# A macaron block's weight preparation on one core: constants between weight tiles, x in four loads, W2 pieces in pair order

## What is computed

```python
x = x + 0.5 * ffn(layernorm(x), W1, W2, W3)
x = x + attention(layernorm(x), qkv_w, ...)   # linear attention with decay, 16 heads of 32, chunks of 128
x = x + 0.5 * ffn(layernorm(x), W1, W2, W3)

def ffn(x, W1, W2, W3):                        # W1, W3: 2048 x 512, W2: 512 x 2048
    hidden = silu(x @ W1.T) * (x @ W3.T)
    return fwht(hidden) @ W2.T                 # fwht: normalised Walsh-Hadamard transform over 2048
```

## Time and profile before

| | |
|---|---|
| median of three runs | 2354.49 us (2353.8 to 2356.52) |
| profiled execution, its own time | 2355.63 us |
| span of its records | 2353.9 us |
| TensorE matmuls busy | 2336.4 us (99%), 12407 instructions |
| VectorE busy | 1232.0 us (52%), 2211 instructions |
| ScalarE busy | 692.4 us (29%), 1164 instructions |
| GpSimd busy | 149.8 us (6%), 126 instructions |
| moved by DMA | 196.83 MB, 299457 packets |

### The profile page before, as it was taken

How to read it: one execution, slowest core, us unless ns; L and a number is a source line. 1 busy time by engine, 2 the same in 40 slices (tenths; PEclk the granted TensorE clock), 3 DMA queues, 4 the chain that set the end, 5 groups by cost and what they waited for, 6 DMA issues and landing times.

```text
span 2353.9 us, 31017 instructions
## 1 busy us (share of the span) xinstructions
PE 2336.4 (99%) x12407; PEld 1120.7 (48%) x12407; DVE 1232.0 (52%) x2211; ACT 692.4 (29%) x1164; POOL 149.8 (6%) x126
## 2 busy tenths in 40 slices
PE   8999999999999999999999999999999999999999
PEld 4444444444544454445444444445444544544444
DVE  6577555654565446546554465544664455445212
ACT  6645233222222222223223222222232213221211
POOL 0190000000000000000000000000000000000000
PEclk9999999999999999999999999999999999999999
DMA  8856622331243212422042223421432224131200
GB/s 218 229 152 175 157 86 64 89 86 50 68 77 107 72 28 82 103 75 64 28 138 51 54 81 90 99 54 28 121 68 85 50 54 99 31 87 36 65 25 19
DMA packets 299457, 196.83 MB, mean 84 GB/s; under 512 B 231600, under 2 KB 256176, under 8 KB 295472
## 3 DMA queue, kind: packets, MB, share of 16 engines
q1 hardware_dynamic: 299024, 194.31, 31.6%
q10 hardware_dynamic: 288, 0.52, 0.1%
HBM read 84.68 MB, written 54.53 MB: 59 GB/s over the span
## 4 chain that ended last, share of the span: by engine, by line
PE 94%; DVE 3%; issue 1%; ACT 1%; DMA 1%; SPq 0%; POOL 0%; DVEq 0%; ACTq 0%; POOLq 0%
PE d_bank L1437 27%; PE l_bank L1417 27%; PE g_bank L1417 26%; PE a_bank L1472 5%; PE a_bank L1532 2%; PE a_bank L1455 2%; PE a_bank L1483 1%; PE a_bank L1514 1%; PE a_bank L1519 1%; PE a_bank L1497 1%; DVE work L1146 1%; DVE work L1126 0%; DMA w1t<-kT 0%; PE a_bank L1521 0%; PE d_bank L1391 0%
## 5 line engine op out<-in xcount | busy, mean ns | idle before, releaser
L1437 PE MATMUL d_bank<-w2t,work 128*128 128x512 f16 x2940 | 671.9, 379 | 0.0
L1437 PEld LDWEIGHTS d_bank<-w2t,work 128*128 128x128 f16 x2940 | 284.7, 98 | 332.4 <-DVE work L1146 0.6
L1126 DVE SCALAR_TENSOR_TENSOR work<-l_bank,l_scale,work 128x512 f32<-128x512 f32 x256 | 191.8, 749 | 468.4 <-PE l_bank L1417 468.4
L1417 PE MATMUL g_bank<-xt,w1t 128*128 128x512 f16 x1536 | 354.1, 380 | 3.6 <-DMA w1t<-kT 3.6
L1417 PE MATMUL l_bank<-xt,w3t 128*128 128x512 f16 x1536 | 352.4, 379 | 0.0
L857 ACT ACTIVATE work<-g_bank,g_scale 128x512 f32<-128x512 f32 x256 | 175.4, 685 | 490.1 <-PE g_bank L1417 488.2
L876 ACT CAST work<-work 128x512 f16<-128x512 f32 x232 | 143.3, 618 | 562.0 <-DVE work L1126 561.1
L1417 PE MATMUL l_bank<-work,w3t 128*128 128x512 f16 x1344 | 308.4, 379 | 0.2 <-DVE work L1126 0.2
L1417 PE MATMUL g_bank<-work,w1t 128*128 128x512 f16 x1344 | 308.3, 379 | 0.0
L1417 PEld LDWEIGHTS g_bank<-xt,w1t 128*128 128x128 f16 x1536 | 148.3, 98 | 177.9 <-DMA w1t<-kT 4.6
L1417 PEld LDWEIGHTS l_bank<-xt,w3t 128*128 128x128 f16 x1536 | 148.1, 98 | 173.0 <-issue 0.2
(11 more groups left out here) (227 smaller groups left out, 1791.1 us busy)
## 6 DMA issues: line engine op xcount, KB each, us to landing
work<-parts_dram SPq DMA_DIRECT2D x192, 128.0 KB, 2.7
x_dram<-work SPq DMA_DIRECT2D x16, 1024.0 KB, 4.2
work<-x_dram SPq DMA_DIRECT2D x11, 1024.0 KB, 6.6
parts_dram<-q_parts SPq DMA_DIRECT2D x32, 256.0 KB, 2.0
parts_dram<-k_parts SPq DMA_DIRECT2D x32, 256.0 KB, 2.2
norm_dram<-cent SPq DMA_DIRECT2D x32, 256.0 KB, 2.0
w2t<-in_L_ffn_W_dram SPq DMA_DIRECT2D x30, 256.0 KB, 3.2
xin<-in_L_attn_x_dram SPq DMA_DIRECT2D x7, 1024.0 KB, 8.4
```

Of the source, the lines that this page charges most:

```text
L1126: nc.vector.scalar_tensor_tensor(out=hfull, in0=l_bank[:], scalar=l_scale[:, j:j + 1], in1=gate, op0=ALU.mult, op1=ALU.mult).then_inc(hful ...
L1417: ins = nc.tensor.matmul(dst[:], wt[:, wp, k, P * j:P * (j + 1)], src[:, xp, k, :], start=(k == 0 and wp == xp), stop=(k == KT - 1 and wp ...
L1437: ins = nc.tensor.matmul(d_bank[t][:], parts[:, hp, P * t:P * (t + 1)], w2t[:, j, wp, :], start=(j == 0 and hp == wp), stop=(j == HT - 1 a ...
```

## The change

The Hadamard constants and `diag` are made by a new step `consts` in three parts, in slots 4, 6 and 8 of the first pass, from other buffers. The next x is loaded in four pieces behind tiles 7, 9, 11 and 13. Its statistics move from slots 7 to 13 to slots 9 to 15, and the six parts of its normalisation from slots 14 to 24 to slots 16 to 26. The scales of chunks 2 and 3 are made one by one, `wsum` 2 comes behind `wprep` 2, `wsum` 3 behind `gate` 0. Batch 0's turns use four banks and four buffers, and `warm` 4 between them is gone. The W2 pieces get new slots, pieces 1 and 2 of each four change places, and pair 0 waits for pieces 0 to 13 only, pair 4 for the last two.

```diff
+        bits_p, bits_j = cent[:, 1, 0:P].bitcast(I32), cent[:, 1, P:2 * P].bitcast(I32)
+        first_cent = zt[:].rearrange("p a k t -> p (a k t)").bitcast(F32).rearrange("p (t d) -> p t d", t=TT)
...
+        turn_bank = a_bank + d_bank[2:4]
...
-        SCALED = [slice(0, 1), slice(1, 2)] + [slice(j, j + 2) for j in range(2, HT, 2)]
+        SCALED = [slice(j, j + 1) for j in range(4)] + [slice(j, j + 2) for j in range(4, HT, 2)]
...
             steps += [("stat", key), ("wscale", 0), ("prep", (key, 0)), ("prep", (key, 1)), ("wprep", 0), ("prep", (key, 2))]
-            steps += [("turn", (key, 0)), ("prep", (key, 3)), ("turn", (key, 1)), ("wprep", 1), ("warm", 4)]
-            steps += [("turn", (key, t)) for t in range(2, TT)] + [("warm", 8), ("wsum", 2), ("wscale", 1), ("wprep", 2), ("wprep", 3)]
-            steps += [("wsum", 3), ("wscale", 2), ("wprep", 4)]
+            steps += [("prep", (key, 3)), ("turn", (key, 0)), ("turn", (key, 1)), ("turn", (key, 2)), ("wprep", 1)]
+            steps += [("turn", (key, 3)), ("warm", 8), ("wscale", 1), ("wprep", 2), ("wsum", 2), ("wprep", 3)]
+            steps += [("wscale", 2), ("wprep", 4)]
             own = {}
             flies = [("fly", (t, st)) for t in range(KT) for st in range(BUTTERFLIES)]
             for t in range(TT):
-                add(own, 7 + 2 * t, [("rows", (("ffn1", 1), t))])
+                add(own, 9 + 2 * t, [("rows", (("ffn1", 1), t))])
             for i, part in enumerate(norm_steps(("ffn1", 1))):
-                add(own, 14 + 2 * i, part)
+                add(own, 16 + 2 * i, part)
+            for part, at in enumerate((4, 6, 8)):
+                add(own, at, [("consts", part)])
             for j in range(HT):
                 steps += [("gate", j)]
                 if j < HT - 2:
                     steps += [("wprep", 2 * j + 5)]
+                if j == 0:
+                    steps += [("wsum", 3), ("wscale", 3)]
                 if j < HT - 4:
                     steps += [("wsum", j + 4)]
                 steps += own.get(2 * j, []) + [("lin", j)]
                 if j < HT - 4 and j % 2:
-                    steps += [("wscale", (j + 5) // 2)]
+                    steps += [("wscale", (j + 7) // 2)]
...
-            splits = (14, 16, 18, 20, 21, 22, 23, 24, 25, 25, 26, 26, 27, 27, 28, 28)
+            splits = (14, 16, 17, 18, 20, 21, 22, 23, 24, 25, 25, 26, 27, 28, 29, 30)
...
+        CHUNK_ORDER = (0, 2, 1, 3)
...
-                    if arg == 5:
-                        sp.dma_start(x_next, x[1].rearrange("(t p) d -> p t d", p=P)).then_inc(x_next_loaded, 16)
+                    if arg in (7, 9, 11, 13):
+                        t = (arg - 7) // 2
+                        sp.dma_start(x_next[:, t, :], x[1, P * t:P * (t + 1), :]).then_inc(x_first[t], 16)
...
-                    t, q = divmod(arg, CHUNKS)
+                    t, q = arg // CHUNKS, CHUNK_ORDER[arg % CHUNKS]
...
+                elif step == "consts":
+                    if arg == 0:
+                        dve.wait_ge(pool_const, 4)
+                        link(nc.vector.tensor_tensor(bits_p, bits_p, bits_j, ALU.bitwise_and))
+                        link(nc.vector.tensor_scalar(bits_j, bits_p, 4, None, ALU.logical_shift_right))
+                        link(nc.vector.tensor_tensor(bits_p, bits_p, bits_j, ALU.bitwise_xor))
+                        link(nc.vector.tensor_scalar(bits_j, bits_p, 2, None, ALU.logical_shift_right))
+                    elif arg == 1:
+                        link(nc.vector.tensor_tensor(bits_p, bits_p, bits_j, ALU.bitwise_xor))
+                        link(nc.vector.tensor_scalar(bits_j, bits_p, 1, None, ALU.logical_shift_right))
+                        link(nc.vector.tensor_tensor(bits_p, bits_p, bits_j, ALU.bitwise_xor))
+                        link(nc.vector.tensor_scalar(bits_p, bits_p, 1, None, ALU.bitwise_and))
+                    else:
+                        nc.vector.tensor_copy(hadamard_f32, bits_p).then_inc(dve_const, 1)
...
-                            pe.wait_ge(w2_turned[b], 16 * KT * CHUNKS // 4)
+                            pe.wait_ge(w2_turned[b], 16 * (KT if b < 2 else KT - 1))
...
                         pe.wait_ge(w2_final_lo, 2 * (i - 3))
+                        if i == 4:
+                            for b in (2, 3):
+                                pe.wait_ge(w2_turned[b], 16 * KT)
...
                     key, t = arg
-                    b = take(step, arg)
+                    b, _ = filled(step, arg)
                     pe.wait_ge(ln_norm, TT * NORM[key] + (t + 1))
                     for k in range(KT):
-                        ins = nc.tensor.transpose(a_bank[b][:, P * k:P * (k + 1)], cent[:, t % 3, P * k:P * (k + 1)], ident[:])
+                        ins = nc.tensor.transpose(turn_bank[t][:, P * k:P * (k + 1)], first_cent[:, t, P * k:P * (k + 1)], ident[:])
```

More of the change, by code:

```diff
@@ L768, in _ @@
             nc.scalar.activation(tiny[:, 15:16], ident[:, 0:1], ACT.Silu)
-            act.wait_ge(dve_const, 1)
-            squares = [(dve_const, 1)]
+            squares = []
             def sum_squares(v, out, done):
-                act.wait_ge(*squares[-1])
+                if squares:
+                    act.wait_ge(*squares[-1])
                 nc.scalar.activation(junk[:], v, ACT.Square, accum_out=out).then_inc(done, 1)
@@ L964, in inverse_norm @@
                                                ALU.mult, ALU.add)
-            dve.wait_ge(pool_const, 4)
-            ip, ij = junk[:, 2 * P:3 * P].bitcast(I32), junk[:, 3 * P:4 * P].bitcast(I32)
-            link(nc.vector.tensor_tensor(ip, ip, ij, ALU.bitwise_and))
-            for shift in (4, 2, 1):
-                link(nc.vector.tensor_scalar(ij, ip, shift, None, ALU.logical_shift_right))
-                link(nc.vector.tensor_tensor(ip, ip, ij, ALU.bitwise_xor))
-            link(nc.vector.tensor_scalar(ip, ip, 1, None, ALU.bitwise_and))
-            nc.vector.tensor_copy(hadamard_f32, ip).then_inc(dve_const, 1)
-            dve.wait_ge(dve_const, 1)
-            nc.vector.tensor_scalar(hadamard[:, 0, :], hadamard_f32, -2.0, 1.0, ALU.mult, ALU.add)
-            nc.vector.tensor_scalar(hadamard[:, 1, :], hadamard_f32, 2.0, -1.0, ALU.mult, ALU.add).then_inc(dve_const, 1)
-            link(nc.vector.memset(diag[:], 0.0))
-            for h in range(HG):
-                nc.vector.memset(diag[HD * h:HD * (h + 1), HD * h:HD * (h + 1)], SCORE_SCALE)
+            dve.wait_ge(pool_const, 2)
             for step, arg in STEPS:
@@ L986, in _ @@
                     n = f.n
+                elif step == "consts":
[12 more added lines that the diff above has]
+                        nc.vector.tensor_copy(hadamard_f32, bits_p).then_inc(dve_const, 1)
+                        dve.wait_ge(dve_const, 1)
+                        nc.vector.tensor_scalar(hadamard[:, 0, :], hadamard_f32, -2.0, 1.0, ALU.mult, ALU.add)
+                        nc.vector.tensor_scalar(hadamard[:, 1, :], hadamard_f32, 2.0, -1.0, ALU.mult, ALU.add).then_inc(dve_const, 1)
+                        link(nc.vector.memset(diag[:], 0.0))
+                        for h in range(HG):
+                            nc.vector.memset(diag[HD * h:HD * (h + 1), HD * h:HD * (h + 1)], SCORE_SCALE)
                 elif step == "wscale":
@@ L1151, in _ @@
                     if kind == "ffn1":
-                        if batch == 0:
-                            dve.wait_ge(x_first[t], 16)
+                        if batch < 2:
+                            dve.wait_ge(x_first[t], 16 * (batch + 1))
                         else:
-                            dve.wait_ge(*((x_next_loaded, 16 * batch) if batch < 4 else (x_loaded, 16 * batch)))
+                            dve.wait_ge(*((x_next_loaded, 16 * (batch - 1)) if batch < 4 else (x_loaded, 16 * batch)))
                     elif kind == "qkv":
@@ L1234, in _ @@
                         dve.wait_ge(ln_lo, TT * (m - 1) + t)
-                    to = centred if m else cent[:, t % 3]
+                    to = centred if m else first_cent[:, t]
                     if key[0] == "qkv":
```

12 lines of the change are left out of this document (6 added, 6 removed).

## The result

The changed kernel took 2359.64 us, the median of 19 runs (2358.55 to 2360.81), against 2354.49 for the kernel before in as many runs on the same chip: ratio 1.002, 95% interval 1.0013 to 1.0027. That is 5.1 us slower. The profiled execution has a span of 2358.9 us against 2353.9. Both profiled executions are 1.0 to 1.1 us above the medians (2360.68 and 2355.63), so the two traces can be compared term by term, but a wait that only some executions have can be in them.

The account below looks back on a forecast made before the run. TensorE, busy 2336.4 of 2353.9 us, was taken as the bound. Terms -4.2 - 5.0 + 10.9 + 1.7 = +3.4 us on the median of 2354.49 gave 2357.9 us, range 2353.5 to 2362.0.

Parts of the forecast that it names:

- the likeliest case: Second pass: `gate` 0 stalls 10.9 us for the transpose behind the W2 loads; 2357.9 us in all, chance 58%.
- Parts 1 and 2: First pass: x in four loads ends the `gate` 3 stall and slow clock, `lin` 1 starts 0.5 later; gain 4.2 us.
- Constants: First pass, VectorE: 3.66 us of constants ahead of `lin` 2, 3 and 4 fit and cost nothing, 0.3 us otherwise.
- Part 3: End of second pass: W2 pieces in new slots let `lin` 15 and pair 0 start on time; gain 5.0 us.
- by `lin` 10 both orders hold the same work: Second pass, VectorE: one more W2 piece stands behind `lin` 8, but old and new slots are level by `lin` 10.
- Part 4: Second pass, `gate` 0: normalisation two slots later puts its transpose behind 4.8 MB; stall 10.9, clock 1.7, loss 12.6 us.
- The rule weighed: Transpose before `gate` 0: about 2.0 us plus bytes at 436 GB/s lands it at 110.1, sum 2352.
- my row: Transpose before `gate` 0: lands at 115.9, from s's landing at 114.9 plus 1.0 us.
- the early drain: Before `gate` 0: rows and s don't hold the transpose, landing 112.3, stall 7.3; 2354.3 us, no change; chance 8%.
- the transpose that isn't held: Before `gate` 0: the transpose is issued ahead of the W2 loads, only gains left; 2345.3 us; chance 8%.
- The deeper backlog: Before `gate` 0: transpose lands at 117.3, clock at 1.2 GHz for two stretches; +6.5, 2361.0 us; chance 26%.

Follow-up runs that it names:

- the first run: The changed kernel with the last split of batch 1's normalisation in slot 25 in place of 26; 2349.18 us, ratio 0.9978.
- the run with the rows behind: The changed kernel with only the three rows and s issued behind the last split's transpose, W2 loads still ahead of it; 2357.48 us, ratio 1.0011.

## Why the prediction was right

The forecast of 2357.9 us was 1.7 below the median of 2359.64, inside its range, and the likeliest case is the one that happened. The sign and the place were right. That the number came so near is in part luck: the gains were taken 0.6 + 1.1 = 1.7 us too large and the loss 1.7 us too large, which cancels; what is left is a term of 1.7 us that was missing.

- **Parts 1 and 2** (gain 4.2): 3.6 in this trace. The wait for `gate` 3 went, as said. `lin` 0 waited 1.1 us for tile 1, of which the forecast says nothing: its ScalarE part stands behind the third turn and the tile is issued at 15.57 in place of 14.92. `lin` 1 came at 26.32 and not 25.75; VectorE's hfull 0 behind the scales of chunk 3 was the bound, as named. The size also rested on one execution whose wait, with its slow clock, was worse than in others: alone, x in four loads gave 2.2 us, not 4.7.
- **Constants:** nothing waits for them, as said.
- **Part 3** (gain 5.0): 3.9. The failed step is "by `lin` 10 both orders hold the same work". In the new slots VectorE does 4, 5, 7 and 9 pieces ahead of hfull 9 to 12, in the old ones 3, 4, 6 and 8; only ahead of hfull 13 both have 12. The extra piece falls in the time in which GpSimd is at work and a piece can cost VectorE 1.75 us in place of 0.75. VectorE falls behind and stays so until the butterflies end; with pieces 2 to 12 back in the old slots most of it went. `lin` 15 and pair 0 were on time, as said.
- **Part 4** (loss 12.6): 9.6 + 1.3 = 10.9; alone 11.8. The mechanism held in each trial. The landing was predicted 12.3 us behind the transpose's issue (115.9 for 103.57) and came 10.0 behind it. I took s's 11.8 us from the trace of before, which were 9.9 in the changed kernel, and added 1.0 for the transpose, which landed 0.7 behind s. Nor is the transpose's issue where the time goes: moved 2.8 us earlier it lands 2.1 earlier, because the bytes ahead have become fewer.
- **The rule weighed** (the Trainium skill, "DMA: Bandwidth & Descriptors", Anatomy of one DMA) gave an estimated 110.1 for the landing on the axis of before. That page of the Trainium skill gives the fit for single DMAs issued by GpSimd; the estimate put it to thirteen in SyncE's queue. The measured 110.9 counts from W2 loads issued at 93.08, so it is 110.9 + 3.0 = 113.9 there: between the rule (3.8 us early) and my row (2.0 us late).
- **Missing:** 1.7 us behind pair 0. I held that what is won or lost before pair 0 stays until the end. It did in eleven of the twelve runs, within 0.3 us; in the profiled executions of the changed kernel and of the first run the first residual came late. VectorE began it 42.2 us behind down 0 there and TensorE waited 1.5, so it was needed at 40.7; before, it began at 40.5. That slack of 0.2 us stands in no list of waits.
- **The rivals:** the early drain and the transpose that isn't held are ruled out by the order of issue and by the run with the rows behind. The deeper backlog was wrong in its mechanism: the landing was earlier, not later. The measured time is still nearer to its 2361.0 than to the forecast, 1.4 against 1.7 us; that is chance, since neither had the wait behind pair 0.

## What to carry to other kernels

A step's place in a list that several engines walk is also its place in the DMA queue: before moving it by a slot, read what the issuing engine has between the two places, and count its bytes. Gains ahead of a stage whose other engines are paced by something else (here GpSimd's butterflies and the load of qkv_w) are partly given back there, so the second trace to read is that of the stage behind. And a stall that is priced from one profiled execution should first be looked for in a second one.

## What the runs showed of the hardware

- A DMA transpose behind 4.8 MB of loads in the same queue landed 10.0 us after its issue, the quickest of the others into zt 3.2; with 4.0 MB ahead and issued 2.8 us earlier, 10.7.
- TensorE's clock was granted at 0.50, 1.2 GHz, from inside the long idle stretches on; in front of `gate` 3 in the kernel before it was still 1.00 when the work resumed after 2.8 us, and fell behind it. Behind stalls of 9.6, 7.7 and 9.6 us the first `gate` cost 1.3, 2.0 and 2.3 us more; behind idle times of 2.2 and 1.3 us in front of `gate` 3 it cost nothing, behind one of 2.8 it cost 1.7.
- VectorE's operations on 128x512 with two inputs in SBUF took 0.7 to 1.8 us beside GpSimd's butterflies, 1.75 in most of the back-to-back ones, and 0.68 to 0.75 without them; those with one input in PSUM took 0.74 either way.
- Instruction fetches of 16 KB share the DMA engines with the data: a transpose that one fell into landed 1.2 to 1.7 us later (seven traces; 3.3 us at most without). 28 more instructions of TensorE (as the page counts them) moved the fetch by 5 us, where 3 were expected at the 0.11 us per instruction of the down products; why is open.
